# First loads of two attention stages issued inside the feed-forward stages ahead of them, and later stages' weights with them

## What is computed

```python
x = x + _L0_ffn_ref(...)     # 8 experts, top 2, relu
x = x + _L1_xattn_ref(...)   # 16-head attention to the context
x = x + _L1_attn_ref(...)
x = x + _L1_ffn_ref(...)     # 8 experts, top 2, swiglu
x = x + _L2_xattn_ref(...)   # single-head attention to the context
x = x + _L2_attn_ref(...)    # an MLP with a projection
```

## Time and profile before

| | us |
|---|---|
| median of three runs | 2862.82 (2861.77 to 2863.46) |
| the profiled execution | 2862.94 |
| its span, first to last instruction | 2861.0 |
| PE busy | 2563.2 (90% of the span) |
| DVE / ACT / POOL busy | 1789.2 / 1631.0 / 1403.2 |
| mean granted clock of PE | 0.935 of 2.4 GHz |

### The profile page before, as it was taken

The page is one execution under the profiler, slowest core; times in us unless marked ns, Lnnn a source line. Parts: engine busy times, 40 slices in busy tenths (PEclk is TensorE's granted clock), DMA queues, the critical chain, the costliest instruction groups (busy, mean ns, idle before and its releaser), DMA issues. The chain is left out here.

```text
span 2861.0 us, 43942 instructions
## 1 busy us (share of the span) xinstructions
PE 2563.2 (90%) x16307; PEld 2152.8 (75%) x16307; DVE 1789.2 (63%) x3737; ACT 1631.0 (57%) x2861; POOL 1403.2 (49%) x1112
## 2 busy tenths in 40 slices
PE   5999999587999999999977788796999999999767
PEld 4899998376999999999966666584677777777547
DVE  7888874545555555555534445616888888888472
ACT  4888885334766666666633243433666666666333
POOL 1877774111766666666610052204656666666140
PEclk9999999788999999999987998797999999999885
DMA  3323321013011111111001151202000000000000
GB/s 110 105 72 106 95 71 36 14 30 88 24 42 29 35 36 36 36 36 35 13 6 45 50 153 31 60 1 78 18 20 24 13 24 25 13 24 2 3 1 8
DMA packets 222574, 117.83 MB, mean 41 GB/s; under 512 B 21368, under 2 KB 217632, under 8 KB 222368
## 3 DMA queue, kind: packets, MB, share of 16 engines
q1 hardware_dynamic: 222368, 115.11, 14.6%
HBM read 100.39 MB, written 13.64 MB: 40 GB/s over the span
## 5 line engine op out<-in xcount | busy, mean ns | idle before, releaser
L846 POOL TENSOR_TENSOR L_xattn_held<-L_xattn_held,L_xattn_shift 128x512 f32<-128x512 f32 (+1 forms) x613 | 762.9, 1292 | 291.3 <-ACT L_xattn_shift L766 290.9
L564 PEld LDWEIGHTS L_xattn_acc<-L_xattn_rows,L_xattn_held 128*128 128x128 f32 (+2 forms) x5120 | 618.5, 192 | 34.7 <-DVE L_xattn_mixed L949 9.1
L564 PE MATMUL L_xattn_acc<-L_xattn_rows,L_xattn_held 128*128 128x129 f32 (+2 forms) x5120 | 628.0, 276 | 5.5 <-DVE L_xattn_mixed L949 5.5
L970 DVE TENSOR_TENSOR L_xattn_running<-L_xattn_ring,L_xattn_running 128x512 f32<-128x512 f32 (+1 forms) x384 | 264.0, 688 | 268.8 <-PE L_xattn_ring L546 257.1
L756 ACT ACTIVATE L_xattn_held<-L_xattn_held 128x512 f32<-128x512 f32 (+2 forms) x640 | 400.4, 631 | 0.2
L1612 POOL TENSOR_TENSOR L_xattn_projected<-L_xattn_along,L_xattn_crossed 128x512 f32<-128x512 f32 (+1 forms) x256 | 271.5, 1071 | 257.6 <-DVE L_xattn_crossed L1679 255.5
L749 ACT COPY L_xattn_held<-L_xattn_ring 128x512 f32<-128x512 f32 (+1 forms) x416 | 243.3, 585 | 227.9 <-DVE L_xattn_running L970 193.3
L544 PE MATMUL L_xattn_ring<-L_xattn_queries_hi,L_xattn_keys_hi 128*128 128x512 f32 (+2 forms) x640 | 280.9, 439 | 3.4 <-DVE L_xattn_keys_lo L874 2.0
L546 PE MATMUL L_xattn_ring<-L_xattn_queries_hi,L_xattn_keys_lo 128*128 128x512 f32 (+2 forms) x640 | 253.4, 396 | 0.0
L545 PE MATMUL L_xattn_ring<-L_xattn_queries_lo,L_xattn_keys_hi 128*128 128x512 f32 (+2 forms) x640 | 252.8, 395 | 0.0
L1319 PE MATMUL L_xattn_sums<-L_xattn_probT,L_xattn_rows 128*128 128x256 f32 (+2 forms) x896 | 243.6, 383 | 0.6 <-ACT L_xattn_mixed L1501 0.6
(11 more groups left out here) (575 smaller groups left out, 4822.7 us busy)
## 6 DMA issues: line engine op xcount, KB each, us to landing
L_xattn_raw<-in_ctx SPq DMA_DIRECT2D x16, 768.0 KB
context_normalised<-L_xattn_fresh SPq DMA_DIRECT2D x16, 768.0 KB
L_xattn_rows<-context_normalised SPq DMA_DIRECT2D x16, 768.0 KB
L_xattn_fresh<-in_ctx SPq DMA_DIRECT2D x16, 768.0 KB
L_xattn_rows<-in_ctx SPq DMA_DIRECT2D x16, 768.0 KB
L_xattn_staged<-in_ctx SPq DMA_DIRECT2D x16, 768.0 KB
L_xattn_xhat<-context_normalised SPq DMA_DIRECT2D x16, 768.0 KB
L_ffn_w<-in_L_ffn_W SPq DMA_DIRECT2D x2, 896.0 KB, 5.4
```

The costliest lines, as they stand in the source:

```text
L564: mm = nc.tensor.matmul(acc[:, c // 2, c % 2 * WIDE:(c % 2 + 1) * WIDE], held[0:n, u % 2, k, c * P:(c + 1) * P], rows[0:n, b % 2, k, :], s ...
L846: nc.gpsimd.tensor_tensor(tile, tile, shift[0:keys_of_tile[k]], ALU.subtract).then_inc(shifted, 1)
L970: seen = nc.vector.tensor_tensor(most, bank, most, ALU.max)
```

## The change

Two objects hold tiles that live across a feed-forward and the attention stage behind it. `FirstLoads` holds `fresh`, `wq_rows` and `wk_rows` of the 16-head stage; `Opening` holds `staged` and the weights of the single-head stage. Each has a `load` that the feed-forward's SP program calls behind its own weights (`load_next`). `Ahead.load` is split: its 14 weight transfers go into `Opening.load`, and the ten into `up` stay behind `during(0, 0)`. The memset of `fresh` is gone. In the single-head stage PE turns the whole of pair 0 ahead of the latents, into three banks, and ACT alone keeps the eight chunks, the first of them ahead of the square roots. Each object is one more `Stage` to clear.

```diff
 # column_attention_stage
-            move_context(raw[:, 0] if normed else fresh, w_ctx, 0, ctx_loaded[0])
             if normed:
+                move_context(raw[:, 0], w_ctx, 0, ctx_loaded[0])
...
-            load(wq_rows[:], wq_src, w_loaded)
-            load(wk_rows[:], wk_src, w_loaded)
...
-            pe.wait_ge(cleared, 2)
             if not normed:
                 for n in range(len(CTX_CHUNKS)):
                     first(n)
+            pe.wait_ge(cleared, 2)
             pe.wait_ge(w_loaded, LOADS)
...
-            act.wait_ge(cleared, 2)
+            if normed:
+                act.wait_ge(cleared, 2)
...
+            act.wait_ge(cleared, 2)
             keep_turned_act(nc, act, yT, [acc[:, 0], acc[:, 1]], y_turned, 1, yT_kept)
...
-            else:
-                nc.gpsimd.memset(fresh[:, CT - 1, :], 0.0)
 # single_head_stage
-        ACT_FIRST, ACT_PAIR = 4 + 1, 4 + 1 + 2
-        DVE_FIRST, DVE_PAIR = 4, 4 + 2
+        ACT_FIRST, ACT_PAIR = 1, 4 + 1 + 2
+        DVE_FIRST, DVE_PAIR = 0, 4 + 2
+
+        first_banks = (score[:, 2 * BANK:3 * BANK], score[:, 3 * BANK:4 * BANK], sums[:])
...
-            for dst, src in ((wq, "Wq"), (wk, "Wk"), (wv, "Wv")):
-                sp.dma_start(dst[:], w[src]).then_inc(w_loaded, 16)
-            with nc.allow_non_contiguous_dma("bias column"):
-                sp.dma_start(bq[:], column(w["bq"])).then_inc(w_loaded, 16)
-            load_staged(0, 0)
-            sp.dma_start(bv_rows[:], w["bv"].partition_broadcast(P)).then_inc(bias_loaded, 16)
-            load_staged(1, 1)
             during(0, 0)
-            core.ahead.load(sp, weights(core.w, "L2_attn"), weights(core.w, "L3_attn"), weights(core.w, "L3_ffn"))
+            core.ahead.load_up(sp, weights(core.w, "L3_attn"))
...
             turn.then_inc(w_turned, 1)
+            def first_context(n):
+                h, c = ALL_CTX[n]
+                if n >= len(first_banks):
+                    pe.wait_ge(first_kept, n - len(first_banks) + 1)
+                bank = first_banks[n % len(first_banks)]
...
+                turn.then_inc(first_full, 1)
+            pe.wait_ge(staged_loaded[0], 64)
+            for n in range(len(ALL_CTX)):
+                first_context(n)
             turn_tiles_pe(nc, pe, core.ident[:], y[:], lane_bank[0:2], y_ready, 1, y_turned, by_halves=True)
...
-            turn_context(0, 0, ALL_CTX)
             make_queries(0)
+            pe.wait_ge(first_kept, len(ALL_CTX))
...
+            keep_first(0)
             normalize_halves_act(nc, act, core.eps(EPS_5), TILES, square, stats, var_ready, std_ready, 0)
+            for n in range(1, len(ALL_CTX) - 2):
+                keep_first(n)
             act.wait_ge(w_turned, 1)
             nc.scalar.copy(wT[:].rearrange("p n d -> p (n d)"), score[:, 0:2 * P]).then_inc(w_kept, 1)
+            for n in range(len(ALL_CTX) - 2, len(ALL_CTX)):
+                keep_first(n)
             keep_turned_act(nc, act, yT, lane_bank[0:2], y_turned, 1, yT_kept)
...
-                if isinstance(pair, int) and pair < 2:
-                    pool.wait_ge(act_full, ACT_FIRST * (pair + 1))
+                if isinstance(pair, int) and pair == 0:
+                    pool.wait_ge(first_full, len(ALL_CTX))
+                elif isinstance(pair, int) and pair == 1:
+                    pool.wait_ge(act_full, ACT_FIRST + 5)
 # moe_stage: behind the last weight transfer on SP
+                load_next(sp)
+class Opening:
+    def load(self, sp):
+        for dst, src in ((self.wq, "Wq"), (self.wk, "Wk"), (self.wv, "Wv")):
+            sp.dma_start(dst[:], self.w[src]).then_inc(self.w_loaded, 16)
+        self.load_staged(sp, 0, 0)
...
+        self.load_staged(sp, 1, 1)
+        self.core.ahead.load_weights(sp, weights(self.core.w, "L2_attn"), weights(self.core.w, "L3_attn"),
+                                     weights(self.core.w, "L3_ffn"))
+class FirstLoads:
+    def load(self, sp):
+        whole = CTX // P * P
+        src = self.core.w["ctx_1024"][0]
+        sp.dma_start(self.wq_rows[:], self.w["W_q"]).then_inc(self.w_loaded, 16)
+        sp.dma_start(self.wk_rows[:], self.w["W_k"]).then_inc(self.w_loaded, 16)
+        sp.dma_start(self.fresh[:, 0:whole // P, :], src[0:whole].rearrange("(k p) d -> p k d", p=P)).then_inc(self.ctx_loaded[0], 16)
+        sp.dma_start(self.fresh[0:CTX - whole, whole // P, :], src[whole:CTX]).then_inc(self.ctx_loaded[0], 16)
 # build
+        with ExitStack() as beside:
+            core.first_loads = FirstLoads(core, beside, weights(w, "L1_xattn"))
+            STAGES["L0_ffn"](core, w)
+            STAGES["L1_xattn"](core, w)
+        STAGES["L1_attn"](core, w)
         with ExitStack() as loading:
             core.ahead = Ahead(nc, ctx, loading)
-            STAGES["L2_xattn"](core, w)
+            with ExitStack() as beside:
+                core.opening = Opening(core, beside, weights(w, "L2_xattn"))
+                STAGES["L1_ffn"](core, w)
+                STAGES["L2_xattn"](core, w)
             STAGES["L2_attn"](core, w)
```

More of the change, by code:

```diff
@@ L270, in column_attention_stage @@
         rows = s.sb("rows", [P, 2, KT, WIDE])
-        fresh = s.sb("fresh", [P, CT, D])
+        fresh = s.sb("fresh", [P, CT, D]) if normed else first_loads.fresh
         keys_hi, keys_lo = s.sb("keys_hi", [P, 2, COLS], F32R), s.sb("keys_lo", [P, 2, COLS], F32R)
@@ L305, in column_attention_stage @@
         w_turned, w_kept = s.sem("w_turned"), s.sem("w_kept")
-        ctx_loaded, rows_loaded = ([s.sem(f"{n}{i}") for i in range(2)] for n in ("ctx_loaded", "rows_loaded"))
+        rows_loaded = [s.sem(f"rows_loaded{i}") for i in range(2)]
+        ctx_loaded = [s.sem(f"ctx_loaded{i}") for i in range(2)] if normed else first_loads.ctx_loaded
         tile_done, tile_seen, tile_kept = s.sem("tile_done"), s.sem("tile_seen"), s.sem("tile_kept")
@@ L417, in _ @@
                         load_rows(b + 1)
-        GAINS, LOADS, LATE_LOADS = (16 * loads[done] for done in (gains_loaded, w_loaded, late_loaded))
+        GAINS, LATE_LOADS = 16 * loads[gains_loaded], 16 * loads[late_loaded]
+        LOADS = 16 * loads[w_loaded] if normed else first_loads.W_LOADS
         QUADS_OF = R // 4
@@ L1758, in single_head_stage @@
         stats = s.sb("stats", [P, 4, TILES])
-        staged = s.sb("staged", [P, 2, 2, CT, D])
+        staged = opening.staged
         rows = s.sb("rows", [P, 2, 2, CT, D])
@@ L1809, in _ @@
         def _(sp):
[L1810 to L1814, removed]
[L1815 removed]
             def during(pair, parity):
                 sp.wait_ge(rows_ready, pair + 1)
[L1820 to L1828 removed]
+                opening.load_staged(sp, pair + 2, parity)
             during(0, 0)
[L1830 removed]
+            core.ahead.load_up(sp, weights(core.w, "L3_attn"))
             with sp.Fori(0, (PAIRS - 2) // 2 - 1) as j:
@@ L1834, in _ @@
             during(PAIRS - 3, 1)
-        LOADS = 4
         @block.tensor
@@ L1845, in _ @@
             turn.then_inc(w_turned, 1)
+            def first_context(n):
[3 more added lines that the diff above has]
+                bank = first_banks[n % len(first_banks)]
+                c0, size_of = CHUNKS[c]
+                for k in range(c0 // P, -(-(c0 + size_of) // P)):
+                    size = tile_of_keys[k][1]
+                    turn = nc.tensor.transpose(bank[:, k * P - c0:k * P - c0 + size], staged[0:size, 0, h, k, :],
+                                               core.ident[0:size, 0:size])
+                turn.then_inc(first_full, 1)
+            pe.wait_ge(staged_loaded[0], 64)
+            for n in range(len(ALL_CTX)):
+                first_context(n)
             turn_tiles_pe(nc, pe, core.ident[:], y[:], lane_bank[0:2], y_ready, 1, y_turned, by_halves=True)
@@ L2224, in _ @@
                 sp.dma_start(b2_sb[:], b2).then_inc(w2_loaded[1], 16)
+                if load_next is not None:
+                    load_next(sp)
         gate_loads = 2 if bg is not None else 1
@@ new lines, with __init__ @@
+class FirstLoads:
+    def __init__(self, core, ctx, w):
+        s = Stage(core.nc, ctx, "first_loads")
+        self.core, self.w = core, w
+        self.fresh = s.sb("fresh", [P, -(-CTX // P), D])
+        self.wq_rows, self.wk_rows = s.sb("wq_rows", [P, 1024]), s.sb("wk_rows", [P, 1024])
+        self.w_loaded, self.ctx_loaded = s.sem("w_loaded"), [s.sem(f"ctx_loaded{i}") for i in range(2)]
+        self.W_LOADS = 16 * 2
+    def load(self, sp):
[5 more added lines that the diff above has]
+        sp.dma_start(self.fresh[0:CTX - whole, whole // P, :], src[whole:CTX]).then_inc(self.ctx_loaded[0], 16)
```

75 lines of the change are left out of this document (50 added, 25 removed).

## The result

The changed kernel takes 2842.7 us in the median (2842.47 to 2843.57, four runs), beside 2863.14 (2861.77 to 2863.78, four runs) of the kernel before: 20.4 us less, ratio 0.9928 (95% interval 0.9913 to 0.9943). The profiled execution took 2842.9, its span 2841.0.

A forecast was written before the change was run, and what follows sets the result against it. It took the stretches in which every engine waits for a first load as what can be won, not PE's 90% busy share. -5.7 - 5.5 - 6.95 + 0.9 = -17.25 us against 2862.94 gave 2845.7; own range 2843.3 to 2848.5, outer 2842.5 to 2853.5.

The forecast's parts named there:

- part 4: Costs elsewhere: two more `Stage` clears at 0.46 each add 0.9 us; transfers under the feed-forwards costed at nothing.
- the cheaper clears: Behind both attention stages: two added clears cost 0.7 us instead of 0.9, one reason for the range's lower end.
- Part 1: Start of the 16-head stage: waits for `fresh` and both weights removed, ACT sets the end; 5.7 us less.
- my upper price: 16-head start: PE transposes at 0.27 us each, the low-clock price, so sixteen weight transposes end at 663.2.
- Part 2: Start of the single-head stage: waits for biases, weights and pair 0 removed; scores 5.5 us earlier (4.4 to 6.6).
- The longer price of a table load: Single-head start: the skill page's 1.38 us drain on top of the 1.28 us load; would give 4.1 instead of 5.5.
- Part 3: Third step of the single-head stage: 14 of 24 issues leave SP's queue, pair 3's stall goes; 6.95 us less.
- Pair 3 late again: Single-head third step: SP meets `up`'s wait or the transfer needs over 10.3 us; 2852.6, 12 in 100.
- the hidden starts: Both attention starts: something behind them, such as POOL's subtraction chain, takes up the shift; near 2863.8, 3 in 100.
- The new wait on ACT: Both attention starts: low clock throughout and the page's drain cost 4.0 us together; 2849.7, 8 in 100.
- the feed-forwards wait for their weights: Both feed-forwards: new transfers delay their own weights, up to 20 and 6.3 us; 2871.9, 5 in 100.
- wrong above all if a feed-forward grew: Sign named for the profile after: feed-forward windows should show more GB/s and the same length.

The follow-up runs named there:

- before_again: The kernel before, unaltered, run again as a second sample of its stages; 2863.53 us.
- start16_back: Changed kernel with the 16-head stage's first loads issued at that stage's own start again; 2852.89 us, ratio 0.9961 against the kernel before.
- next_before_own: Changed kernel with the swiglu feed-forward's `load_next` issued ahead of the weights of experts 1 to 7; 2856.5 us, ratio 0.9973 against the kernel before.
- ahead_back: Changed kernel with the 14 weight transfers back behind `during(0, 0)`; 2845.9 us, ratio 0.9936 against the kernel before.
- start16_only: Kernel before with only `FirstLoads` and its `load_next` in the relu feed-forward added; 2851.75 us, ratio 0.9969.
- roots_first: Changed kernel with ACT's first copy moved between the single-head stage's two square roots; 2840.95 us, ratio 0.9921 against the kernel before; repeated at 2838.78 and 2838.43.

## Why the prediction was right, and where it was off

**The sum.** Forecast -17.25; the two attention stages (-5.9 and -11.8) and the relu feed-forward (-0.2, chance, as under part 4) gave -17.9 in the profiled pair. The swiglu feed-forward gave +1.4 and all other stages together -3.5: -20.0, the difference of the spans (2861.0 to 2841.0). So of the 3.0 us by which the time came out under the forecast, 0.7 are of the terms, and most of the rest lies in stages that the change does not touch. That part is luck: the touched stages with both feed-forwards gave -16.6, and had the others stood still, 2846.4 would have been measured. Of the prediction's own reasons for the lower end of its range, only the cheaper clears came about.

**Part 1**, forecast -5.7. Measured at the scores: -6.27 in the profiled pair, -5.5 to -6.3 between any of the profiles. ACT set the end, as forecast: weight copies end at 663.32 and the product follows at 663.38. The product starts 6.51 us after the block where I had 7.05, and the mis-sized step is before the copies: ACT's last rounding ended at 4.44 (661.08 + 0.23 - 656.87) where I had 4.75, and PE's last weight transposes at 5.8 where my upper price gave 6.7. The four copies at 0.54 were right. The clock reached its upper level 5.1 us after PE's first transpose, where the forecast took over 5.2 from the profile before. That was a reading of one start: in `before_again` it was 3.0 us, in `start16_back` 12.4.

**Part 2**, forecast -5.5. Measured -5.44 (16.48 to 11.04), and 11.02 to 11.04 four times. The path was as written, first copy, table load, square roots, copies, latents, fold, queries, at the low clock to the latents: PE turned them 7.19 us after the start, where the forecast had 7.1 to 7.8. That the total fits so well is partly luck. By the prediction's own terms (latents from 1633.7 or 1634.4, then 3.1 and 0.9) the scores come at 1637.7 to 1638.4, and it wrote 1637.5; what made up for it is that these last terms took 3.85 us and not 4.0 (1633.46 - 1629.61). And the clock could have given more: with the same code in this start, the scores came at 10.08, 10.08 and 9.17 in `start16_back`, `next_before_own` and `ahead_back`, so part 2 was worth 5.4 to 7.3 us. No run has part 2 alone done or undone; its price is read at this start, 16.1 to 16.6 us in the four profiles without it and 8.7 to 11.0 in the ten with it. The longer price of a table load falls: the square roots' ACTIVATE started 0.02 us after the load's 1.28 us were over (1624.58 + 1.28 = 1625.86, next row 1625.88), in the place where the path waits for it. The Trainium skill ("ScalarE: Activation LUTs", section What ACT_TABLE_LOAD costs) adds 1.38 us of drain to each switch; the trace disagrees at both ends of this load, ahead of which ACT's copy ended at 1624.56.

**Part 3**, forecast -6.95. Measured -6.96 in the step (19.44 to 12.48), and -6.9 of the stage with the part done alone. Pair 3's load was forecast right behind POOL's second copy; it was issued at 1652.85, 0.19 us after that copy ended (1644.99 + 7.67). It was not late again: from issue to need lay 10.4 us (1660.31 + 2.92 - 1652.85).

**Part 4**, forecast +0.9. The gaps behind the attention stages grew by 0.39 (0.93 to 1.32) and 0.38 (0.88 to 1.26), so 0.77 for two clears, where I had 0.46 each. `start16_only` has the one clear and shows the one gap grown (1.32, and 0.87 behind the single-head stage). The gap ahead of the 16-head stage went from 1.83 to 1.56, which is the -0.2 of the relu feed-forward above, but it is not the change's: the kernel before had 1.55 itself in its second profile.

```profile
655.80 0.87 DVE L128 BATCH_NORM_STATS2 L_xattn_square<-all_lat 128x6 f32<-128x128 f32 x4 [1.55 <-PEq L54]
```

So the 0.46 for a clear, half of 1.82 less 0.90, was worked out from a gap that does not repeat; from 1.55 it would have been 0.33, and 0.38 was measured. Two pairs, the stage's weights and the 14 transfers sum to 6.16 MB and not 6.0; nothing hangs on it.

**The rivals.** Pair 3 late again and the hidden starts are excluded by the above. The new wait on ACT is there, 1.13 us of PE at L1848, but within the forecast's own path. That the feed-forwards wait for their weights did not happen; `next_before_own` shows that such a wait can be had, by the order of the issues, with a price of 12 us between medians.

**What was wrong.** I had written that I was wrong above all if a feed-forward grew, and one did: the swiglu one by 1.1 to 1.4 us in all four profiles of the changed kernel. It was costed at nothing for want of a wait, and there is none. The third 10 us of that stage, before, after, and in `roots_first`, which loads the same there:

```profile
1536.79:1546.79 10.00, 6.88 (x28) 5.39 (x27) 5.84 (x19) 2.65 (x5) 0.00 (x0) 0.83 0.01 2
```

```profile
1531.29:1541.29 10.00, 6.87 (x24) 5.30 (x23) 5.43 (x18) 2.65 (x5) 0.00 (x0) 0.72 1.08 309
```

```profile
1534.72:1544.72 10.00, 6.88 (x28) 5.38 (x27) 5.83 (x19) 2.65 (x5) 0.00 (x0) 0.83 1.08 307
```

The clock is 0.83, 0.72 and 0.83. Of the eight profiles with all these loads behind the stage's own (DMA share 1.02 to 1.10 in this stretch), six ran it at 0.71 or 0.72, and their stage took 110.9 to 111.1; two, this one and `start16_back`, ran it at 0.83 and took 109.8, the old length. The five profiles with fewer loads there all ran at 0.83 and took 109.7 to 109.9. So the loads do not lengthen the stage by themselves, but go with the lower clock more often than not. The two forms part earlier than these windows, where the clock first rises in the stage, between 16 and 18 us after its start; in the changed kernel and in `roots_first`:

```profile
1527.29:1529.29 2.00, 2.00 (x7) 1.57 (x6) 0.69 (x1) 0.75 (x3) 0.00 (x0) 0.59 1.20 289
```

```profile
1530.72:1532.72 2.00, 2.00 (x6) 1.59 (x5) 0.69 (x1) 0.72 (x3) 0.00 (x0) 0.52 1.19 291
```

The clock in this stretch was 0.59 to 0.65 in the six long profiles and 0.50 to 0.54 in all the others. Where it rose some tenths of a microsecond sooner, it also fell sooner, and was back at its upper level only 31 us after the stage's start instead of 28. The DMA share is nearly the same in the two rows (1.20 and 1.19). What makes it rise sooner, and whether the loads have a part in it, is not settled.

**What stays open.** Why the clock falls once more in L3_xattn in some profiles and not in others, and why L2_attn takes its fast form in `start16_only` and three times in `roots_first`. No edit tried here was made to steer it, so some 3 us of the measured 20.4, and 3.5 to 6 us in two of the experiments, are told by where they lie and not by a cause.

## What to carry to other kernels

A stage that stands still for its first load can take it from the stage in front, if the issue sits behind that stage's own weights on the queue; the wrong order cost 12 of 20 us here. Look past the starts for loads that are late because the queue's engine was issuing something else: that one step (19.4 instead of 12.5 us) was worth more than either start, and it is partly the same stall that an earlier start removes, so price the two together. Where an effect of a few microseconds is wanted, compare the stages one by one and not the total alone: untouched stages moved by as much as a part did.

## What the runs showed of the hardware

- PE's granted clock gives a stage two lengths with the same instructions: L2_attn 65.3 to 65.7 or 59.7 to 61.9 us, L3_xattn 751.6 to 752.1 or 753.6 to 754.5, the swiglu feed-forward 109.7 to 109.9 or 110.9 to 111.1. Which one is met differed between profiles of one kernel (L3_xattn in the changed kernel) and between versions that have the same code there (L2_attn).
- The single-head start in its new form reached its scores in 8.7, 9.2, 9.5, 10.1 or 11.0 us in profiles of versions that differ little there. The clock was still at 0.51 between 6 and 9 us after the start in the changed kernel, and already at 0.88 between 3 and 6 us in the profile of `roots_first` shown above.
- One more object to clear between two stages costs 0.38 to 0.39 us.
- Single issues on SP can take long: 5.15 us in the changed kernel and 5.45 in `next_before_own` for a transfer of the experts' weights, where most take 0.43. It goes with what is ahead of the issue: the last 32.5 KB of a context batch took 0.72 us to issue behind one transfer of 768 KB, and 2.77 behind two (kernel before, 1650.77 and 1651.95).
